# Chosen prototype weights turned by a DMA together with the weighed products, the search for the two nearest prototypes placed elsewhere, and the distances' roots by logarithm

## The chip, the cores and the metric

The kernel runs on one core of one Trainium2 chip. The metric is the device time of one execution in microseconds, from the median of several runs. The engines are TensorE (PE, matmuls; PEld its weight loads), VectorE (DVE), ScalarE (ACT), GpSimd (POOL) and SyncE (SP, which here issues most DMAs). Each runs its own instructions in order and waits on semaphores for the others.

## The reference, cut to what matters

Two layers, each a cross attention and a feed-forward part, on `x` of 64 x 256 tokens of 256 values:

```
x = x + tanh(g_xattn[0]) * L0_xattn(layernorm(x), ctx, ctx)
x = x + tanh(g_ffn[0])   * L0_ffn(layernorm(x))             # mixture of experts
x = x + tanh(g_xattn[1]) * L1_xattn(layernorm(x), ctx, ctx) # 16 heads of 64, 77 keys
x = x + tanh(g_ffn[1])   * L1_ffn(layernorm(x))
```

The change is in the last line. For each token `xf` and the 32 prototypes:

```
d2 = x2 + p2[None, :] - 2.0 * (xf @ prototypes.T)
dists = sqrt(maximum(d2, 0))
w = softmax(-dists / t); topw, topi = top_k(w, 2); topw = topw / sum(topw)
for tslot in range(2):                       # the two nearest prototypes
    h = einsum('nri,ni->nr', B[idx], xf)     # rank 16
    y = einsum('nor,nr->no', A[idx], h) + bias[idx]
    out = out + topw[:, tslot] * y
```

Of the softmax only the two nearest count, so the kernel needs their distances' gap alone.

## The kernel before

The second layer is `attention_ffn_phase`. It works on 64 batches of two tiles of 128 tokens (`TPB` is 2; h = 0 is the even tile of a batch and h = 1 the odd one). Its bodies are written out for the first and the last batches, and in a loop of 16 batches between them. A tile passes through a pipeline of eight steps; in the body of tile t each engine works at several tiles in a fixed order, which is the order written in `body` of each engine (lines 1207, 1338, 1458, 1607). Between the engines stand semaphores; `need(engine, semaphore, value)` is a wait.

For tile t the attention's scores are made. For tile t-1 they are made to exponentials (ScalarE) and half sums (GpSimd `softmax_sums`, L1143). For t-2 follow the inverse sums (VectorE, L1534) and the normalising (GpSimd, L1153). For t-3 TensorE turns the probabilities in three groups (L1442), ScalarE writes their high half (L1243) and VectorE their low half (`split_lo`, L1527), and attention adds the products with the values (L1454). For t-4 the second layer norm is made (ScalarE), split in two half-precision parts, the low one by GpSimd (`normed_low`, L1170), and turned by a DMA (L1089). For t-5 TensorE multiplies it with all 32 x 16 columns of `B` and with the prototypes (`low`, two banks); ScalarE copies the products, VectorE makes the distances' variable part (`dots`). Then, still in that body and as its last work but one, VectorE searches the two nearest of t-5 (`nearest_two`, `nearest_index`, L1569 to L1579).

For t-6 ScalarE makes the two squared distances (`square_gaps`, L1293); GpSimd adds a tiny number, takes the root as a power of 0.5, subtracts, and takes a power for the weights' ratio (`top_weights`, L1180). VectorE makes the two weights, compares a row of indices with each index found (`pick`, twice, L1658), and adds the two picks to `wsel`: three copies of the 32 weights side by side (L1665). For t-7 GpSimd multiplies `low` with the weights (`weigh`, L1194), ScalarE and GpSimd split the product in two halves (`hw_parts`, L1330 and L1175), and SyncE turns them by one DMA transpose of 8 blocks of 128 x 128 (L1095). `wsel` is turned on its own: TensorE transposes it into a bank (L1502), ScalarE copies 96 rows as half precision (L1384), and VectorE makes of the third copy the remainder (L1638): `wselT`. For t-8 TensorE multiplies `hwT` with `A` (12 matmuls) and `wselT` with the biases (L1486), and VectorE adds the result to the rows (L1627).

Five banks of the matrix engine's output memory go round among these uses (`Ring`, L84; `uses`, L981). Before TensorE fills a bank it waits for whoever read that bank's last use (`freed`, L998). The second half of `low` in an even tile takes the bank of the first group of the turned probabilities of the same tile. The second query block of an even tile takes the bank of the first half of `low`.

Once in a batch GpSimd also makes the low half of the normalised rows of the batch ahead (`rows_low`, L1165), at the start of an even tile.

The functions that the change touches:

Of the kernel before, what the change touches and what calls it, by code (L numbers as in the profile page):

```python
# [15 lines left out]
P = 128  # L16
# [67 lines left out]
class Ring:  # L84
# [3 lines left out]
    def __init__(self, uses, banks, first, last, steady):  # L88
        self.banks, self.steady = banks, steady
        self.flat, self.at_use = [], {}  # L90
        for i in range(first, last):
            for name in uses(i):
                self.at_use[i, name] = len(self.flat)
                self.flat.append((i, name))
        self.per = len(uses(steady))
        assert self.per % banks == 0
        tails = [uses(i)[-banks:] for i in (steady - 1, steady)]
        assert tails[0] == tails[1]

    def fill(self, i, name):  # L100

        n = self.at_use[i if isinstance(i, int) else self.steady, name]
        k = n // self.banks + 1
        return n % self.banks, k if isinstance(i, int) else (i - self.steady) * (self.per // self.banks) + k

    def before(self, i, name):

        n = self.at_use[i if isinstance(i, int) else self.steady, name] - self.banks
# [600 lines left out]
def attention_ffn_phase(nc, ctx, psum, const, src, src_rows, dst, keys, values, wq, score_scale, ffn, experts):  # L709
# [39 lines left out]
    SUM_STEPS, TOP_STEPS = 2, 4  # L749
# [28 lines left out]
    wsel_zero, euler_set, decay_ready = sem("wsel_zero"), sem("euler_set"), sem("decay_ready")  # L778
# [15 lines left out]
    gap_ready, ln_log, ln_root, more_ready, first_weight = sem("gap_ready"), sem("ln_log"), sem("ln_root"), sem("more_ready"), sem("first_weight")  # L794
# [5 lines left out]
    low_ready, hw_ready, hw_hi, hw_lo, wselT_hi, wselT_ready, out_ready = (  # L800
        sem("low_ready"), sem("hw_ready"), sem("hw_hi"), sem("hw_lo"), sem("wselT_hi"), sem("wselT_ready"),
        sem("out_ready"))
# [159 lines left out]
    wsel = sb("wsel", [P, P])  # L962
    wselT = sb("wselT", [BIAS_ROWS, P], F16)
    low = [sb(f"low{p}", [P, LOW]) for p in range(2)]
    hw = sb("hw", [P, LOW])
    hw_parts = sb("hw_parts", [P, 2, LOW], F16)
    hwT = [sb(f"hwT{p}", [P, 2 * LC, P], F16) for p in range(2)]
# [9 lines left out]
    def uses(i):  # L977

        names = []
        for h in range(TPB):  # L980
# [8 lines left out]
            names += of(7, [("wselT", h)])  # L989
# [6 lines left out]
    ring = Ring(uses, WORK, 0, END, BODIES)  # L996

    def freed(i, use):  # L998
# [11 lines left out]
        return (wselT_ready, t - 6) if what == "wselT" else (out_ready, t - 7)  # L1010
# [34 lines left out]
    def _(sp):  # L1045
# [45 lines left out]
        def turn_weighed(t, p):  # L1091
# [3 lines left out]
            sp.dma_start_transpose(hwT[p][:, :, :], flat(hw_parts[:, :, :])).then_inc(hwT_in[p], 16)  # L1095
# [30 lines left out]

        load_x(2, 2, 0)
# [9 lines left out]
    def _(pool):  # L1137
        pool.memset(wsel[:, :], 0.0).then_inc(wsel_zero, 1)
# [55 lines left out]
        def weigh(t, h):  # L1194
# [6 lines left out]
                               wsel[:, 0:NPROTO].unsqueeze(2).broadcast_to([P, NPROTO, RANK]), ALU.mult)\  # L1201
                .then_inc(hw_ready, 1)

        def body(i, u, j):
            for h in range(TPB):
# [23 lines left out]
    def _(act):  # L1229
# [63 lines left out]
        def square_gaps(t, h, u):  # L1293
# [3 lines left out]
            need(act, ysq_done, t + 1)  # L1297
            need(act, more_ready, t)
            act.activation(square[:, :], top[:, 0:2], ACT.Relu, bias=ysq[:, n:n + 1], scale=-1.0).then_inc(gap_ready, 1)
# [30 lines left out]
        def weighed_high(t, u, h, j):  # L1330

            need(act, hw_ready, t + 1)
            if live(t - 1, NT):
                earlier, times = turned_place(8, u, h, j)
                need(act, hwT_in[earlier], (times + 1) * 16)
            act.activation(hw_parts[:, 0, :], hw[:, :], ACT.Copy).then_inc(hw_hi, 1)

        def body(i, u, j):
            for h in range(TPB):
# [14 lines left out]
                if live(t - 6, NT):  # L1354
                    square_gaps(t - 6, h, u)
# [10 lines left out]
                if live(t - 4, NT):  # L1366
# [31 lines left out]
    def _(pe):  # L1398
# [67 lines left out]
        def body(i, u, j):  # L1466
            for h in range(TPB):
# [9 lines left out]
                if live(t - 8, NT):  # L1477
# [3 lines left out]
                    need(pe, wselT_ready, t - 7)  # L1481
# [4 lines left out]
                    filled(nc.tensor.matmul(bank[:, 0:D], wselT[:, :], ffn["bias"][:, :], start=False, stop=True),  # L1486
# [22 lines left out]
        pe.wait_ge(wsel_zero, 1)  # L1509
# [1519 lines left out]
```

## Time and profile before

| | us |
|---|---|
| median of 3 runs | 3023.89 |
| lowest and highest | 3023.6, 3030.8 |
| the profiled execution | 3015.37 |
| its span, first to last instruction | 3013.7 |
| TensorE busy | 2738.8 (91%) |
| VectorE busy | 2461.3 (82%) |
| ScalarE busy | 2199.1 (73%) |
| GpSimd busy | 2084.7 (69%) |

The second layer begins at about 1460 us and goes to the end. All times in the timelines are microseconds from the span's start. A line of a timeline is one or several like instructions: start, duration, engine and line, what is written and read, how many (x), and in brackets how long the engine had been idle before and who ended that. A merged line's duration runs to the end of its last instruction. Instructions of an engine overlap a little: the next often starts before the last one's recorded end. For a small instruction the distance between two starts is what it costs its queue. Names carry a prefix (`a_`), and buffer numbers are left out: some of TensorE's rows name a weight that shares its place.

### The profile page before, as it was taken

To read this page: it belongs to the slowest core of one execution; us is meant where nothing else is said; L and a number is where in the kernel's file an instruction comes from. 1 tells how busy PE (TensorE), PEld (TensorE's weight loads), DVE (VectorE), ACT (ScalarE), POOL (GpSimd) and SP (SyncE) were. 2 spreads that over 40 slices of the span, in tenths; PEclk is the share of its full clock that TensorE was granted. 3 is DMA by queue.
4 is the path that set the end of the run, shared out by engine and by line. 5 is a ranking of instruction groups with operands and counts; after the bars stand their busy time and mean duration, and the time that the engine had idled before them with its cause. 6 is when DMAs were issued, how large, how long until landed. Compare 5 with 4: busy or idle time off the path is not lost.

```text
span 3013.7 us, 96194 instructions
## 1 busy us (share of the span) xinstructions
PE 2738.8 (91%) x31534; PEld 2164.9 (72%) x31534; DVE 2461.3 (82%) x5870; ACT 2199.1 (73%) x5452; POOL 2084.7 (69%) x2777
## 2 busy tenths in 40 slices
PE   3889897899999999789799999999999999999996
PEld 2444444687778777657588888888888888888884
DVE  6787786688888888675589989888888888989884
ACT  2666666677777777575577777788877788778873
POOL 3893000576667666644378888888888888888886
PEclk7999999899999999999899999999999999999998
DMA  5997666223223223632467777677776777767763
GB/s 153 354 352 293 242 256 255 78 78 92 84 80 89 83 81 94 221 101 59 103 144 162 151 152 149 145 152 149 149 142 147 150 151 146 149 149 153 148 132 79
DMA packets 568793, 455.47 MB, mean 151 GB/s; under 512 B 383616, under 2 KB 527600, under 8 KB 555312
## 3 DMA queue, kind: packets, MB, share of 16 engines
q1 hardware_dynamic: 548144, 402.29, 53.2%
q0 software_dynamic: 7328, 23.40, 2.5%
q10 hardware_dynamic: 12960, 25.23, 2.3%
q8 instruction: 195, 3.19, 0.5%
q14 instruction: 166, 1.36, 0.2%
HBM read 235.08 MB, written 148.83 MB: 127 GB/s over the span
## 4 chain that ended last, share of the span: by engine, by line
PE 33%; DVE 10%; issue 4%; POOL 2%; DMA 1%; ACT 1%; SPq 0%; DVEq 0%; POOLq 0%; ACTq 0%
PE banks L150 10%; PE banks L152 9%; PE banks L151 9%; DVE a_pick L1658 2%; PE banks L1450 2%; DVE a_probT_lo L1527 2%; PE banks L1436 2%; DVE a_y L1604 1%; DVE a_rsum L1539 1%; DVE a_stats L1645 1%; DVE a_wtop L1597 1%; PE banks L1502 0%; DVE a_qT_lo L1525 0%; DVE a_smax L1546 0%; POOL a_pn L1160 0%
## 5 line engine op out<-in xcount | busy, mean ns | idle before, releaser
L383 POOL TENSOR_TENSOR a_probT_lo<-a_expT,a_probT_hi 128x512 f16<-128x512 f32 x256 | 291.5, 1160 | 218.4 <-ACT a_probT_hi L466 218.4
L459 ACT ACTIVATE a_expT<-banks,a_top,w_score_scale 128x512 f32<-128x512 f32 (+1 forms) x384 | 272.3, 709 | 152.4 <-PE banks L550 146.0
L1160 POOL TENSOR_TENSOR a_pn<-a_prob,a_rsum 128x1024 f32<-128x1024 f32 (+1 forms) x256 | 310.3, 1233 | 53.3 <-DVE a_rsum L1541 53.2
L1243 ACT ACTIVATE a_qT_hi<-banks 128x512 f16<-128x512 f32 x252 | 149.8, 595 | 210.1 <-PE banks L152 210.1
L150 PE MATMUL banks<-a_xnT,w_q_hi 128*128 128x256 f16 x1024 | 281.9, 275 | 15.8 <-DMA a_xnT<-a_xn_parts 13.9
L150 PE MATMUL banks<-a_vo_front,a_probT_hi 128*128 128x256 f16 x1024 | 279.5, 273 | 9.6 <-DVE a_probT_lo L1527 3.6
L151 PE MATMUL banks<-a_xnT,w_q_hi 128*128 128x256 f16 x1024 | 281.7, 275 | 0.0
L152 PE MATMUL banks<-a_xnT,w_q_lo 128*128 128x256 f16 x1024 | 281.5, 275 | 0.0
L152 PE MATMUL banks<-a_vo_front,a_probT_lo 128*128 128x256 f16 x1024 | 279.3, 273 | 0.0
L151 PE MATMUL banks<-a_vo_front,a_probT_hi 128*128 128x256 f16 x1024 | 279.3, 273 | 0.0
L1243 ACT ACTIVATE a_probT_hi<-banks 128x512 f16<-128x512 f32 (+1 forms) x384 | 193.8, 517 | 42.2 <-PE banks L1450 41.3
L1525 DVE TENSOR_TENSOR a_qT_lo<-banks,a_qT_hi 128x512 f16<-128x512 f32 x252 | 172.3, 684 | 45.5 <-ACT a_qT_hi L1243 40.7
L550 PE MATMUL banks<-ident,a_shifted 128*128 128x128 f32 (+1 forms) x1280 | 204.4, 284 | 5.3
L1527 DVE SCALAR_TENSOR_TENSOR a_probT_lo<-banks,a_probT_hi 128x512 f16<-128x512 f32 (+1 forms) x384 | 206.9, 581 | 0.3 <-ACT a_probT_hi L1243 0.3
L2397 DVE SCALAR_TENSOR_TENSOR kv_vo_out<-banks,kv_vo_out 128x512 f16<-128x512 f32 (+1 forms) x312 | 191.6, 679 | 16.5 <-ACT kv_vo_out L2295 16.5
L1450 PE MATMUL banks<-ident,a_pn 128*128 128x128 f32 (+1 forms) x1280 | 197.6, 278 | 2.0 <-issue 2.0
L659 DVE TENSOR_TENSOR a_shifted<-banks,a_smax 128x1024 f32<-128x1024 f32 (+1 forms) x256 | 192.2, 793 | 3.8
L2295 ACT ACTIVATE kv_vo_out<-banks 128x512 f16<-128x512 f32 (+1 forms) x312 | 172.4, 603 | 29.4 <-DMA vo<-kv_vo_out 22.1
L150 PE MATMUL banks<-w_downT_hi,a_ynT 128*128 128x288 f16 (+1 forms) x512 | 145.0, 283 | 47.5 <-DVE a_probT_lo L1527 45.1
L1199 POOL TENSOR_TENSOR a_hw<-a_low,a_wsel 128x512 f32<-128x512 f32 x128 | 135.4, 1058 | 72.7 <-DVE a_wsel L1665 72.7
L649 DVE TENSOR_REDUCE a_smax<-banks 128x16 f32<-128x1232 f32 x128 | 183.6, 1435 | 2.2 <-PE banks L536 1.9
L1278 ACT ACTIVATE a_prob<-banks,a_third_shift,w_score_scale 128x77 f32<-128x77 f32 x512 | 170.7, 414 | 12.0 <-ACT a_third_shift L1273 0.4
(383 smaller groups left out, 10315.9 us busy)
## 6 DMA issues: line engine op xcount, KB each, us to landing
vo<-kv_vo_out SPq DMA_DIRECT2D x38, 2048.0 KB, 7.8
a_vo_front<-vo SPq DMA_DIRECT2D x128, 512.0 KB
kt<-kv_k_out ACTq DMA_DIRECT2D x9, 2560.0 KB, 15.0
a_k<-kt SPq DMA_DIRECT2D x64, 308.0 KB, 3.4
kv_raw_e<-in_L_ffn_w POOLq DMA_DIRECT2D x16, 1024.0 KB, 8.8
a_x<-in_x SPq DMA_DIRECT2D x64, 256.0 KB, 2.9
a_y<-in_x SPq DMA_DIRECT2D x64, 256.0 KB, 2.7
x<-a_y SPq DMA_DIRECT2D x64, 256.0 KB, 2.8
```

The source lines that it names most:

```text
L150: nc.tensor.matmul(out, lhs[0], rhs[0], start=start, stop=False)
L151: nc.tensor.matmul(out, lhs[0], rhs[1], start=False, stop=False)
L152: return nc.tensor.matmul(out, lhs[1], rhs[0], start=False, stop=stop)
L383: pool.tensor_tensor(probT[b][1][:, first:end, :], expT[b][:, first:end, :], probT[b][0][:, first:end, :], ALU.subtract).then_inc(prob_rea ...
L459: act.activation(expT[1 - h][0:rows, first:end, :], bank, ACT.Exp, bias=top[0:rows, 0:1], scale=weights["score_scale"][0:rows, 0:1]).then_ ...
L550: last = nc.tensor.transpose(bank[0:rows, c * P:(c + 1) * P], shifted[1 - h][:, place:place + rows], ident[:, :])
L659: last = nc.vector.tensor_tensor(shifted[h][:, cols].rearrange("p (r h k) -> p r h k", r=TILES, k=end - first), held_scores[:, :, :, first ...
L1160: last = pool.tensor_tensor(keys_of(pn[h]), e[:, :, first:end].rearrange("p (a c) k -> p a c k", a=outer), rsum[h][:, :].rearrange("p (a c ...
L1243: act.activation(out, bank[:, 0:cols].rearrange("p (c s) -> p c s", c=out.shape[1]), ACT.Copy, scale=scale)\
L1450: last = nc.tensor.transpose(bank[0:rows, c * P:(c + 1) * P], turned, ident[:, :])
L1527: nc.vector.scalar_tensor_tensor(out=lo, in0=bank, scalar=scale, in1=hi, op0=ALU.mult, op1=ALU.subtract)\
L2397: nc.vector.scalar_tensor_tensor(out=vo_out[q][0:m, placed(b), 1, :], in0=product_banks(g, c, b, m), scalar=1.0 / OUT_TOP, in1=vo_out[q][0 ...
```

## The change

1. `wsel` becomes [128, 32], one copy of the weights. ScalarE writes two half-precision copies of it (`wsel_parts[:, 0:2]`) and GpSimd the remainder (`wsel_parts[:, 2]`), right behind the split products in one row `hw_all` of 9 x 128 columns; 32 columns at its end are zeroed once, and SyncE waits for that at its start. The DMA transpose turns 9 blocks in place of 8, and the bias matmul takes its weights from the ninth. TensorE's transpose of `wsel`, ScalarE's copy of it and VectorE's remainder leave. VectorE's `wsel` waits for the last tile's split (`hw_lo`) in place of `wselT_ready` and `hw_ready`.
2. The bank of that transpose stays in the ring as a spare that nobody fills: the next use of the bank waits for the use before the spare.
3. VectorE's search of a tile moves from the end of one body to the next body, behind the three low halves of the probabilities and ahead of the scores' maximum.
4. ScalarE's `square_gaps` moves behind the length of the normed rows (`length2`) and ahead of their high half. Behind that half comes the logarithm of the squares (`log_gaps`), with the tiny number as its bias, and behind the copies of `low` the exponential of half of it (`root_gaps`).
5. GpSimd's `top_weights` loses the addition and the power; it waits for `dist_ready`. It now stands behind `normed_low`.

The core of the diff (the parts of `Ring`, of the semaphores' names and of the tiles' sizes are left out):

```diff
@@ SyncE
-            sp.dma_start_transpose(hwT[p][:, :, :], flat(hw_parts[:, :, :])).then_inc(hwT_in[p], 16)
+            sp.dma_start_transpose(hwT[p][:, :, :], hw_all[:, :]).then_inc(hwT_in[p], 16)
...
+        sp.wait_ge(pad_zero, 1)
@@ GpSimd
-        pool.memset(wsel[:, :], 0.0).then_inc(wsel_zero, 1)
+        pool.memset(hw_all[:, 2 * LOW + BIAS_ROWS:], 0.0).then_inc(pad_zero, 1)
...
             need(pool, hw_hi, t + 1)
+            pool.tensor_tensor(wsel_parts[:, 2, :], wsel[:, :], wsel_parts[:, 0, :], ALU.subtract)
             pool.tensor_tensor(hw_parts[:, 1, :], hw[:, :], hw_parts[:, 0, :], ALU.subtract).then_inc(hw_lo, 1)
...
-            need(pool, gap_ready, t + 1)
-            kept = pool.tensor_tensor(dist[:, :], square[:, :], numbers[:, 2:3].broadcast_to([P, 2]), ALU.add)
+            need(pool, dist_ready, t + 1)
+            gap = pool.tensor_tensor(dgap[:, :], dist[:, 1:2], dist[:, 0:1], ALU.subtract)
             pool.tensor_copy(topf[:, :], topi[:, 0:2]).then_inc(top_ready, 1)
-            step(kept)
-            step(pool.tensor_tensor(dist[:, :], dist[:, :], numbers[:, 1:2].broadcast_to([P, 2]), ALU.pow))
-            step(pool.tensor_tensor(dgap[:, :], dist[:, 1:2], dist[:, 0:1], ALU.subtract))
+            step(gap)
             step(pool.tensor_tensor(late[:, :], decay[:, :], dgap[:, :], ALU.pow))
...
+                if live(t - 4, NT):
+                    normed_low(t - 4)
                 if live(t - 6, NT):
                     top_weights(t - 6)
-                if live(t - 4, NT):
-                    normed_low(t - 4)
@@ ScalarE
+        def log_gaps(t):
+            need(act, gap_squared, t + 1)
+            act.activation(square[:, :], square[:, :], ACT.Ln, bias=numbers[:, 2:3]).then_inc(gap_log, 1)
+        def root_gaps(t):
+            need(act, gap_log, t + 1)
+            need(act, more_ready, t)
+            act.activation(dist[:, :], square[:, :], ACT.Exp, scale=0.5).then_inc(dist_ready, 1)
...
+            act.activation(wsel_parts[:, 0:2, :], wsel[:, :].unsqueeze(1).broadcast_to([P, 2, NPROTO]), ACT.Copy)
             act.activation(hw_parts[:, 0, :], hw[:, :], ACT.Copy).then_inc(hw_hi, 1)
...
-                if live(t - 6, NT):
-                    square_gaps(t - 6, h, u)
                 if live(t - 4, NT):
                     norm2_root(t - 4)
...
                     length2(t - 4, h, u)
+                if live(t - 6, NT):
+                    square_gaps(t - 6, h, u)
+                if live(t - 4, NT):
                     normed_high(t - 4, u, h, j)
+                if live(t - 6, NT):
+                    log_gaps(t - 6)
...
-                if live(t - 7, NT):
-                    bank = full(i, ("wselT", h))
-                    act.activation(wselT[:, :], bank[0:BIAS_ROWS, 0:P], ACT.Copy).then_inc(wselT_hi, 1)
+                if live(t - 6, NT):
+                    root_gaps(t - 6)
@@ TensorE
-                    need(pe, wselT_ready, t - 7)
...
-                    filled(nc.tensor.matmul(bank[:, 0:D], wselT[:, :], ffn["bias"][:, :], start=False, stop=True),
+                    filled(nc.tensor.matmul(bank[:, 0:D], hwT[turned][0:BIAS_ROWS, 2 * LC, :], ffn["bias"][:, :], start=False, stop=True),
                            i, ("ffn", h))
...
-                if live(t - 7, NT):
-                    need(pe, wsel_ready, t - 6)
-                    bank = bank_for(i, ("wselT", h))
-                    filled(nc.tensor.transpose(bank[:, 0:P], wsel[:, :], ident[:, :]), i, ("wselT", h))
@@ VectorE
+                if live(t - 6, NT):
+                    nearest_two(t - 6)
+                    nearest_index(t - 6)
                 if live(t, NT):
                     maximum(t)
...
-                if live(t - 7, NT):
-                    bank, rows = full(i, ("wselT", h)), slice(2 * NPROTO, BIAS_ROWS)
-                    need(dve, wselT_hi, t - 6)
-                    nc.vector.tensor_tensor(wselT[rows, :], bank[rows, 0:P], wselT[rows, :], ALU.subtract)\
-                        .then_inc(wselT_ready, 1)
...
-                    need(dve, wselT_ready, t - 6)
-                    need(dve, hw_ready, t - 6)
-                    nc.vector.tensor_tensor(wsel[:, 0:BIAS_ROWS].rearrange("p (r n) -> p r n", r=3),
-                                            pick[:, 0, :].unsqueeze(1).broadcast_to([P, 3, NPROTO]),
-                                            pick[:, 1, :].unsqueeze(1).broadcast_to([P, 3, NPROTO]), ALU.add)\
-                        .then_inc(wsel_ready, 1)
-                if live(t - 5, NT):
-                    nearest_two(t - 5)
-                    nearest_index(t - 5)
+                    need(dve, hw_lo, t - 6)
+                    nc.vector.tensor_tensor(wsel[:, :], pick[:, 0, :], pick[:, 1, :], ALU.add).then_inc(wsel_ready, 1)
```

## Rows read from the trace of the kernel before

**Rows 1.** The page's first line.

```profile
span 3013.7 us, 96194 instructions
```

**Rows 2.** Busy time by engine in a stretch: length, PE, PEld, DVE, ACT, POOL, clock, DMA.

```profile
1600.00:2900.00 1300.00, 1250.08 (x15296) 1082.09 (x15294) 1155.26 (x3284) 1033.98 (x3096) 1136.15 (x1604) 1.00 0.72 149
```

**Rows 3.** Waits of TensorE from 1600 to 2900 us: total, times, longest.

```profile
PE banks L150 <- DVE a_probT_lo L1527: 41.4, 55, 1.6
```

**Rows 4.** Timeline of TensorE: start, duration, line, output<-input, count, [idle before <-releaser].

```profile
2104.96 0.27 PE L1502 MATMUL banks<-ident,a_wsel 128*128 128x128 f32 x1
...
2111.89 0.27 PE L150 MATMUL banks<-w_upT_hi,a_hwT 128*128 128x256 f16 x1
...
2114.98 0.28 PE L150 MATMUL banks<-w_downT_hi,a_ynT 128*128 128x256 f16 x1 [0.77 <-DVE a_probT_lo L1527]
...
2115.64 0.27 PE L1502 MATMUL banks<-ident,a_wsel 128*128 128x128 f32 x1
2115.99 0.28 PE L150 MATMUL banks<-a_vo_front,a_probT_hi 128*128 128x256 f16 x1
```

**Rows 5.** Timeline of VectorE in the same batch.

```profile
2109.86 0.48 DVE L1604 SCALAR_TENSOR_TENSOR a_y<-banks,out_scale,a_y 128x256 f32<-128x256 f32 x1 [1.43 <-PE banks L152]
...
2111.20 1.71 DVE L1658 TENSOR_SCALAR a_pick<-iota,a_topf,a_wtop 128x32 f32<-128x32 f32 x2
2112.95 0.26 DVE L1665 TENSOR_TENSOR a_wsel<-a_pick 128x96 f32<-128x96 f32 x1
2113.13 0.19 DVE L1574 MAX8 a_top<-a_dots 128x8 f32<-128x32 f32 x1
...
2113.55 0.42 DVE L1539 TENSOR_REDUCE a_rsum<-a_quarter 128x16 f32<-128x256 f32 x1
...
2114.23 1.62 DVE L1527 SCALAR_TENSOR_TENSOR a_probT_lo<-banks,a_probT_hi 128x512 f16<-128x512 f32 x3
```

**Rows 6.** Timeline of GpSimd in the same batch.

```profile
2105.11 1.16 POOL L1178 TENSOR_TENSOR a_hw_parts<-a_hw,a_hw_parts 128x512 f16<-128x512 f32 x1 [0.48 <-ACT a_hw_parts L1336]
...
2107.28 0.19 POOL L1190 TENSOR_TENSOR a_dgap<-a_dist 128x1 f32<-128x1 f32 x1
...
2108.34 0.67 POOL L1173 TENSOR_TENSOR a_yn_parts<-a_yn,a_yn_parts 128x256 f16<-128x256 f32 x1
2108.97 1.30 POOL L1148 TENSOR_TENSOR a_half<-a_prob 128x512 f32<-128x512 f32 x1
...
2111.72 1.15 POOL L1168 TENSOR_TENSOR a_xn_parts<-a_xn,a_xn_parts 128x512 f16<-128x512 f32 x1
```

**Rows 7.** Timeline of ScalarE in the same batch.

```profile
2103.77 0.19 ACT L1291 ACTIVATE a_rstd<-a_vare 128x1 f32<-128x1 f32 x1
2103.86 0.19 ACT L1255 ACTIVATE a_minus_mean<-a_mv 128x2 f32<-128x2 f32 x1
2103.95 0.28 ACT L1256 ACTIVATE a_vare<-a_mv,eps 128x2 f32<-128x2 f32 x1
2104.14 0.28 ACT L1304 ACTIVATE a_shift<-a_minus_mean,a_rstd 128x1 f32<-128x1 f32 x1
...
2106.95 0.26 ACT L1384 ACTIVATE a_wselT<-banks 96x128 f16<-96x128 f32 x1
2107.11 0.59 ACT L1243 ACTIVATE a_qT_hi<-banks 128x512 f16<-128x512 f32 x1
...
2110.32 0.63 ACT L1320 ACTIVATE a_xn_parts<-a_xn 128x512 f16<-128x512 f32 x1
```

**Rows 8.** Timeline of SyncE's queue: transposes of the weighed products, mid-loop and at the end.

```profile
2106.44 1.27 SPq L1095 DMA_TRANSPOSE a_hwT<-a_hw_parts  x1
...
2983.52 1.23 SPq L1095 DMA_TRANSPOSE a_hwT<-a_hw_parts  x1
...
3003.45 1.23 SPq L1095 DMA_TRANSPOSE a_hwT<-a_hw_parts  x1
```

**Rows 9.** Tile hwT, its transposes' time to landing, all 128.

```profile
DMA to landing us min/median/max: 3.0/3.1/6.3
```

More of the change, by code:

```diff
@@ L84, with __init__ @@
 class Ring:
-    def __init__(self, uses, banks, first, last, steady):
-        self.banks, self.steady = banks, steady
+    def __init__(self, uses, banks, first, last, steady, spare=None):
+        self.banks, self.steady, self.spare = banks, steady, spare
         self.flat, self.at_use = [], {}
+        filled = [0] * banks
         for i in range(first, last):
             for name in uses(i):
-                self.at_use[i, name] = len(self.flat)
+                filled[len(self.flat) % banks] += name[0] != spare
+                self.at_use[i, name] = len(self.flat), filled[len(self.flat) % banks]
                 self.flat.append((i, name))
-        self.per = len(uses(steady))
-        assert self.per % banks == 0
+        kept = uses(steady)
+        assert len(kept) % banks == 0
+        start = self.at_use[steady, kept[0]][0]
+        self.per = [sum(name[0] != spare for name in kept[(s - start) % banks::banks]) for s in range(banks)]
         tails = [uses(i)[-banks:] for i in (steady - 1, steady)]
@@ L100, in fill @@
     def fill(self, i, name):
-        n = self.at_use[i if isinstance(i, int) else self.steady, name]
-        k = n // self.banks + 1
-        return n % self.banks, k if isinstance(i, int) else (i - self.steady) * (self.per // self.banks) + k
+        n, k = self.at_use[i if isinstance(i, int) else self.steady, name]
+        s = n % self.banks
+        return s, k if isinstance(i, int) else (i - self.steady) * self.per[s] + k
     def before(self, i, name):
-        n = self.at_use[i if isinstance(i, int) else self.steady, name] - self.banks
+        n = self.at_use[i if isinstance(i, int) else self.steady, name][0] - self.banks
+        while n >= 0 and self.flat[n][1][0] == self.spare:
+            n -= self.banks
         if n < 0:
@@ L961, in attention_ffn_phase @@
     pick = sb("pick", [P, 2, NPROTO])
-    wsel = sb("wsel", [P, P])
-    wselT = sb("wselT", [BIAS_ROWS, P], F16)
+    wsel = sb("wsel", [P, NPROTO])
     low = [sb(f"low{p}", [P, LOW]) for p in range(2)]
     hw = sb("hw", [P, LOW])
-    hw_parts = sb("hw_parts", [P, 2, LOW], F16)
-    hwT = [sb(f"hwT{p}", [P, 2 * LC, P], F16) for p in range(2)]
+    TURNED = 2 * LC + 1
+    hw_all = sb("hw_all", [P, TURNED * P], F16)
+    hw_parts = hw_all[:, 0:2 * LOW].rearrange("p (s n) -> p s n", s=2)
+    wsel_parts = hw_all[:, 2 * LOW:2 * LOW + BIAS_ROWS].rearrange("p (r n) -> p r n", r=3)
+    hwT = [sb(f"hwT{p}", [P, TURNED, P], F16) for p in range(2)]
     first_x = [sb(f"first_x{n}", [P, D]) for n in range(FIRST_X)]
@@ L988, in uses @@
             names += of(5, [("low", h, n) for n in range(LU)])
-            names += of(7, [("wselT", h)])
+            names += of(7, [("spare", h)])
             names += prep(4)
@@ L994, in uses @@
         return names
-    ring = Ring(uses, WORK, 0, END, BODIES)
+    ring = Ring(uses, WORK, 0, END, BODIES, "spare")
     def freed(i, use):
@@ L1009, in freed @@
             return y_ready, t - 2
-        return (wselT_ready, t - 6) if what == "wselT" else (out_ready, t - 7)
+        return out_ready, t - 7
     def bodies(eng, body):
@@ L1200, in weigh @@
                                low[h][:, :].rearrange("p (n r) -> p n r", n=NPROTO),
-                               wsel[:, 0:NPROTO].unsqueeze(2).broadcast_to([P, NPROTO, RANK]), ALU.mult)\
+                               wsel[:, :].unsqueeze(2).broadcast_to([P, NPROTO, RANK]), ALU.mult)\
                 .then_inc(hw_ready, 1)
@@ L1297, in square_gaps @@
             need(act, ysq_done, t + 1)
+            act.activation(square[:, :], top[:, 0:2], ACT.Relu, bias=ysq[:, n:n + 1], scale=-1.0).then_inc(gap_squared, 1)
+        def log_gaps(t):
[3 more added lines that the diff above has]
+            need(act, gap_log, t + 1)
             need(act, more_ready, t)
-            act.activation(square[:, :], top[:, 0:2], ACT.Relu, bias=ysq[:, n:n + 1], scale=-1.0).then_inc(gap_ready, 1)
+            act.activation(dist[:, :], square[:, :], ACT.Exp, scale=0.5).then_inc(dist_ready, 1)
         def norm2_shift(t):
```

15 lines of the change are left out of this document (6 added, 9 removed).

## The prediction

> **What bounds the kernel now.** The profiled execution took 3015.4 us, its span is 3013.7 [rows 1]; the median of the runs shown is 3023.9, 8.5 above it. The sums below are made in the profiled execution, and the 8.5 is added at the end. The change lies in the second layer's loop, 64 batches of two tiles. I read the busy times of a stretch in the middle of that loop first: of 1300 us TensorE is busy 1250, at a granted clock of 1.00 (its 2.4 GHz level), all others less [rows 2]. So TensorE sets the pace except where it waits. The waits come next: one large group, 41.4 us in 55 waits, so one in each batch of 1300 / 55 = 23.6 us, released by the VectorE line that writes the probabilities' low halves [rows 3].
>
> The timeline of one batch shows where. I call the tile whose `low` products come at 2104 the odd tile (h = 1), the next one the even tile (h = 0). In the even tile the second half of `low` starts after 0.77 us of idleness. The turn of `wsel` follows at 2115.64 and attention at 2115.99, 0.35 later; attention needs the last low half, which ends at 2114.23 + 1.62 = 2115.85. In the pipeline a matmul or a turn takes 0.11 us (six from 2114.98 to 2115.64; a row's 0.27 is the latency), so 0.24 of the 0.35 is waiting. Together TensorE loses 0.77 + 0.24 = 1.01 us a batch to VectorE [rows 4].
>
> Then backwards along VectorE [rows 5]. It idles 1.43 us before the residual at 2109.86, so its lateness begins after that. The two picks begin at 2111.20 and end only at 2112.91. On GpSimd the low half of the next batch's rows runs 2111.72 to 2112.87 [rows 6]: the second pick ends 0.04 after it. So the loop that sets the end of a batch is: GpSimd's `top_weights`, `normed_low`, `softmax_sums`, `rows_low`; then pick, `wsel`, search, inverse sums, low halves on VectorE; then attention on TensorE. GpSimd in turn was released by ScalarE at 2105.11, after an idle 0.48, and ScalarE by TensorE's third turn of probabilities.
>
> **The change, part by part.**
>
> *Search moved behind the low halves.* From its first instruction, 2113.13, to the inverse sums, 2113.55, it holds VectorE 0.42 us, in the loop. It now runs after the low halves, on no one's path to attention: 0.42 gained. In its new place it stands in front of the maximum and of the reading of the prototype products. Both follow the same chain, so what is gained ahead of the low halves covers it: they come 0.86 earlier by the sum below and 0.42 later by the search. If that cover is gone, TensorE's second query block, which takes the bank of these products, waits.
>
> *`wsel` from 96 to 32 columns.* 0.26 us now; the inverse sums' 256 columns take 0.42 [rows 5], which makes 1.0 ns a column and 0.06 for 64. Bounds 0 and 0.13 (half); I take 0.06.
>
> *GpSimd.* The addition and the power leave; in the loop they take 2106.22 to 2107.28, from the end of `weighed_low` at 2105.11 + 1.11 to the subtraction [rows 6]. The low half of `wsel`, 32 columns, comes in front of `weighed_low`: between nothing and the 0.19 of the subtraction; I take 0.15. `normed_low` moves ahead of `top_weights`, which changes no sum but starts its transpose 2 us earlier. Without a wait, `softmax_sums` would start 1.06 - 0.15 = 0.9 earlier. But `top_weights` now waits for ScalarE's root.
>
> *ScalarE.* Between the third high half and the root: the square leaves its old place and returns before the low products' copies, no change. Added are the copy of `wsel` to two halves, 64 columns, and the logarithm. A logarithm of two columns takes 0.19 in the queue (2103.95 to 2104.14), an exponential 0.09 (2103.77 to 2103.86) though it lasts 0.19; the copy I put at 0.15, by the copy of `wselT`, 0.16 in the queue (2106.95 to 2107.11) for 128 columns; it could be 0.09 to 0.30 [rows 7]. The root takes the place of that copy: it starts at 2106.95 + 0.15 + 0.19 = 2107.29 and ends at 2107.48. GpSimd's subtraction then starts at 2107.53, with 0.05 for the release; from there to the end of the group is 2108.34 - 2107.28 = 1.06, so `softmax_sums` starts at 2108.59 in place of 2108.97: 0.38 gained, and most of the 0.9 is lost in the wait. Queued behind the waiting subtraction are only `top_weights` and `softmax_sums`. If the copy and the logarithm cost their full durations (0.26, 0.28) the gain falls to 0.18; if the release is late too, to nothing or a loss of 0.1. The other end is the 0.9 of a root that is there in time. ScalarE as a whole gets 0.15 + 0.19 + 0.09 - 0.16 = 0.27 later, so the high half that `rows_low` needs ends at 2110.95 + 0.27 = 2111.22; GpSimd reaches `rows_low` at 2111.72 - 0.38 = 2111.34. It just does not wait.
>
> *TensorE.* Two turns of `wsel` leave, 0.22 a batch. The even tile's lies before the attention, which waits for VectorE anyway; the odd tile's lies outside the loop above (it leaves TensorE at the third turn of probabilities and comes back at the even tile's attention). So while the stall stays they are worth nothing. They raise the most that can be had: 1.01 + 0.22 = 1.23 a batch. The bias matmul and the banks' order stay; the spare bank frees nothing that was waited for.
>
> *VectorE's low half of `wselT`* leaves too. It lies outside the loop, since VectorE catches up anyway in its 1.43 of idleness: nothing.
>
> *The transpose of nine blocks in place of eight.* It is issued at 2106.44, lands 3.1 later, 2109.5, and TensorE uses it at 2111.89 [rows 4, 8, 9]: 2.3 us of slack. One block more makes at most 3.1 x 9/8 = 3.5, and 0.15 later for GpSimd's addition. Nothing; without cover it would be 1 us for each us.
>
> *Start and end.* The wait of SyncE for the memset at the start replaces others, under 1 us either way. At the end the last tiles run one after another, 6.6 us each (four issues from 2983.52 to 3003.45 [rows 8]). There each tile gets longer by the copy 0.15, GpSimd's subtraction 0.15 and the ninth block 0.2: 0.5, five times, 2.5 us. Bounds 0 and 6.
>
> **Sum.** 0.42 + 0.06 + 0.38 = 0.86 us a batch. It counts in some 61 batches of 64, without those in which the pipeline fills and drains: 52.5 us. Less 2.5: 50 faster. 3015.4 - 50 = 2965.4, and with the 8.5 between profile and median, 2974.
>
> **The rivals.**
>
> *A pick gets ahead of `rows_low`.* GpSimd starts `rows_low` by my numbers 0.12 after its input is there. If ScalarE's additions are a little dearer, or GpSimd a little faster, there is a gap between its two instructions in which the second pick runs first. Then VectorE gains nearly the whole of `rows_low`'s 1.15 on top, the stall is gone, and TensorE's 1.23 is the gain: 61 x 1.23 - 2.5 = 72.5, 2951. For it speaks how narrow the 0.12 is; against it that `softmax_sums`, which holds the first pick back in the same way, would have to end before the input of `rows_low` is there.
> The Trainium skill (SBUF — State Buffer, "Who interferes with whom") says that such a VectorE instruction and a GpSimd one exclude each other and whoever issues first holds the pair for its whole length. By that rule, and the trace agrees with the 0.04 above, the order of the two decides and not their lengths.
>
> *The gain on GpSimd does not come.* The chain search, square, logarithm, root, subtraction, power crosses three engines inside one tile. If the root comes 0.4 later than I have it, only 0.48 a batch is left: 61 x 0.48 - 2.5 = 27, 2997. For it speaks that I know ScalarE's additions only from neighbours.
>
> *Slower: the ninth block.* An odd number of blocks might not go at the price of the others. The place is the odd tile's transpose, used by the even tile's `ffn`. From there to attention TensorE needs 2115.64 - 2111.89 - 0.77 = 2.98. Attention is later than now only if the landing takes more than 2115.99 - 2.98 - 2106.59 = 6.4 us. The longest landing so far is 6.3 [rows 9]; with 9/8 of that, 7.1 each time, it is 0.7 a batch slower, 61 x 0.7 + 2.5 = 45, 3069. Against it: the median landing is 3.1 and the lowest 3.0, so hardly anything moves it now.
>
> *The relief is filled by other waits* (the query bank, a bank freed by `ffn`'s addition): within 0.3%, 3024.
>
> **How the numbers follow.** Forecast 0.46, own range 2962 to 2986 (the copy and the logarithm at their two ends). Pick ahead 0.28; no gain on GpSimd 0.16; filled by other waits 0.05; slower 0.05. 0.3% is 9 us, about what a measurement of this kernel can tell from no change. The first three are faster by more: 0.90; the same 0.05; slower 0.05. The range takes in the first three with their bounds: 2945 is 64 x 1.23 = 79 with no loss at the end; 3004 is 61 x 0.38 - 2.5 = 20.5, where GpSimd's part turns to a loss of 0.1. So 2945 to 3005.
>
> **What would show it.** In the profile after: TensorE's wait for the low halves smaller than 41.4 (by my sum 1.23 - 0.86 = 0.37 a batch are left, ahead of attention rather than in `low`); a batch 0.86 us shorter; the search between low halves and maximum; `softmax_sums` starting 1.1 after the root ends; the second pick still ending with `rows_low`. It is wrong if a batch gets more than 1.1 shorter (the pick was ahead), if GpSimd starts `softmax_sums` no earlier after the third high half than now, or if TensorE shows waits for the transposed weights.

## The result, and the profile after

| | before, us | after, us |
|---|---|---|
| median | 3023.95 | 2976.54 |
| lowest and highest | 3023.6, 3030.8 | 2971.54, 2977.84 |
| the profiled execution | 3015.37 | 2975.93 |
| its span | 3013.7 | 2973.9 |

The ratio is 0.9839, with a 95% interval of 0.9825 to 0.9853. The kernel became 1.6% faster. The forecast was 2974, with a range of 2945 to 3005. The medians differ by 47.4 us and the two profiled executions by 39.4. The same kernel on another chip gave 0.9851 (0.9834 to 0.9869).

The first line of the page, and TensorE's wait for the low halves from 1600 to 2860 us (total, times, longest), to be set beside [rows 1, 3]:

```profile
span 2973.9 us, 95792 instructions
```

```profile
PE banks L156 <- DVE a_probT_lo L1541: 25.4, 103, 0.5
```

The wait fell from 41.4 to 25.4 us, and it is now met about twice in a batch. TensorE's timeline shows both places, the second half of `low` and attention. The first row is the third turn of probabilities in the odd tile, where ScalarE and GpSimd start from:

```profile
2086.26 0.43 PE L1470 MATMUL banks<-ident,a_pn 128*104 128x128 f32 x2
...
2098.20 0.29 PE L158 MATMUL banks<-w_downT_hi,a_ynT 128*128 128x288 f16 x1
2098.88 0.28 PE L156 MATMUL banks<-w_downT_hi,a_ynT 128*128 128x256 f16 x1 [0.39 <-DVE a_probT_lo L1541]
...
2099.43 0.27 PE L158 MATMUL banks<-w_downT_hi,a_ynT 128*128 128x256 f16 x1
2099.88 0.28 PE L156 MATMUL banks<-a_vo_front,a_probT_hi 128*128 128x256 f16 x1 [0.18 <-DVE a_probT_lo L1541]
```

In `low` 0.39 us of idleness are left of the 0.77 [rows 4]. From the last matmul of `low` to attention it is 0.45, so 0.34 of waiting beside the 0.11 that a matmul takes, where it was 0.24. Together that is 0.73 a batch, from 1.01.

The idle times 0.77 and 0.39 begin only at the recorded end of the matmul ahead, so its latency hides a part of the waiting. That matmul in the kernel before:

```profile
2113.93 0.29 PE L152 MATMUL banks<-w_downT_hi,a_ynT 128*128 128x288 f16 x1
```

From start to start it is 2114.98 - 2113.93 = 1.05 before and 2098.88 - 2098.20 = 0.68 now, of which such a matmul takes 0.12 in the pipeline. So TensorE loses 0.93 there before and 0.56 now, and with attention 1.17 a batch before and 0.90 now. The difference hardly changes, but the prediction's 1.01, and with it the most that can be had, was 0.16 too small.

VectorE in the same batch, from the residual to the search in its new place:

```profile
2094.13 0.48 DVE L1618 SCALAR_TENSOR_TENSOR a_y<-banks,out_scale,a_y 128x256 f32<-128x256 f32 x1 [1.10 <-PE banks L158]
...
2095.31 0.57 DVE L1611 TENSOR_TENSOR a_wtop<-a_late,a_wtop 128x1 f32<-128x1 f32 x1
2095.91 1.31 DVE L1670 TENSOR_SCALAR a_pick<-iota,a_topf,a_wtop 128x32 f32<-128x32 f32 x2
2097.25 0.19 DVE L1676 TENSOR_TENSOR a_wsel<-a_pick 128x32 f32<-128x32 f32 x1
2097.45 0.42 DVE L1553 TENSOR_REDUCE a_rsum<-a_quarter 128x16 f32<-128x256 f32 x1
...
2098.13 1.62 DVE L1541 SCALAR_TENSOR_TENSOR a_probT_lo<-banks,a_probT_hi 128x512 f16<-128x512 f32 x3
2099.67 0.19 DVE L1588 MAX8 a_top<-a_dots 128x8 f32<-128x32 f32 x1
```

Against [rows 5]: from the end of the picks to the inverse sums it took 2113.55 - 2112.91 = 0.64 and now takes 2097.45 - 2097.22 = 0.23. The line of the farther weight lasts 0.57. In the kernel before it lasted 0.12:

```profile
2111.04 0.12 DVE L1597 TENSOR_TENSOR a_wtop<-a_late,a_wtop 128x1 f32<-128x1 f32 x1
```

GpSimd in the same batch: `normed_low`, the subtraction, the first half sum, the last one, `rows_low`:

```profile
2090.77 0.67 POOL L1181 TENSOR_TENSOR a_yn_parts<-a_yn,a_yn_parts 128x256 f16<-128x256 f32 x1
2091.99 0.19 POOL L1195 TENSOR_TENSOR a_dgap<-a_dist 128x1 f32<-128x1 f32 x1 [0.55 <-ACT a_dist L1316]
...
2093.05 1.30 POOL L1156 TENSOR_TENSOR a_half<-a_prob 128x512 f32<-128x512 f32 x1
...
2095.25 0.62 POOL L1159 TENSOR_TENSOR a_quarter<-a_quarter,a_prob 128x208 f32<-128x208 f32 x1
2095.82 1.15 POOL L1176 TENSOR_TENSOR a_xn_parts<-a_xn,a_xn_parts 128x512 f16<-128x512 f32 x1
```

The farther weight ends when the last half sum has ended (2095.87), the first pick can start only at 2095.91, and `rows_low` has begun at 2095.82. So both picks now stand behind it. They end 0.25 after it; before, only the second stood there and ended 0.04 after it [rows 5, 6].

ScalarE: the copy of `wsel`, the weighed products, the logarithm and its neighbour, the root and its neighbour:

```profile
2088.61 0.24 ACT L1353 ACTIVATE a_hw_all<-a_wsel 128x64 f16<-128x64 f32 x1
2088.76 0.61 ACT L1354 ACTIVATE a_hw_all<-a_hw 128x512 f16<-128x512 f32 x1
...
2090.54 0.28 ACT L1310 ACTIVATE a_square<-a_square,a_numbers 128x2 f32<-128x2 f32 x1
2090.73 0.47 ACT L1274 ACTIVATE a_shift<-a_minus_mean,a_rstd 128x1 f32<-128x1 f32 x2
...
2091.63 0.19 ACT L1316 ACTIVATE a_dist<-a_square 128x2 f32<-128x2 f32 x1
2091.72 0.58 ACT L1250 ACTIVATE a_qT_hi<-banks 128x512 f16<-128x512 f32 x1
```

The copy costs its queue 0.15, the logarithm 0.19, the root 0.09.

The time a batch takes in us, from one odd tile's residual to the next (starts in VectorE's timeline; the residuals in the timelines above are those of even tiles, with the same period in mid-loop), by stretch, and the kernels of the experiments beside it. Batch 1 is the first with a residual in both tiles; during the first 13 VectorE also adds the first layer's expert outputs.

| kernel | start of batch 1 | 1-13 | 14-28 | 29 | 30-43 | 44-59 | 60-63 | rest |
|---|---|---|---|---|---|---|---|---|
| before | 1508.3 | 23.71 | 23.35 | 23.31 | 23.63 | 23.18 | 21.56 | 35.5 |
| after | 1513.6 | 22.58 | 22.83 | 22.80 | 22.99 | 22.62 | 20.45 | 35.8 |
| after, other chip | 1511.2 | 22.58 | 22.83 | 22.80 | 23.00 | 22.62 | 20.55 | 35.7 |
| search back | 1512.9 | 23.27 | 23.18 | 23.16 | 23.47 | 23.02 | 20.56 | 35.7 |
| power back | 1509.9 | 23.16 | 23.10 | 23.07 | 23.29 | 22.88 | 21.12 | 36.6 |
| turns kept | 1510.6 | 22.59 | 22.84 | 22.82 | 23.33 | 22.64 | 20.33 | 35.8 |
| rows later | 1511.7 | 22.41 | 22.52 | 23.19 | 22.84 | 22.35 | 20.18 | 37.2 |
| rows behind picks | 1503.9 | 22.48 | 22.12 | 22.00 | 22.41 | 21.93 | 20.13 | 35.8 |
| turn alone | 1508.8 | 23.47 | 23.45 | 23.41 | 23.71 | 23.28 | 21.26 | 36.6 |
| twelve blocks | 1512.7 | 22.60 | 22.83 | 22.82 | 23.00 | 22.63 | 20.46 | 37.6 |
| rows behind, turns kept | 1514.5 | 22.60 | 22.23 | 22.11 | 22.72 | 22.15 | 20.54 | 35.8 |
| before, rows behind picks | 1509.9 | 23.14 | 22.53 | 22.39 | 22.78 | 22.74 | 21.50 | 34.4 |

From the first column on, the span fell by 45 us: 14.7 in batches 1 to 13, 8.4 in 14 to 29, 17.9 in 30 to 59, 4.4 in the last four, and 0.4 back at the end. Ahead of that column nothing was changed, and yet it differs by up to 11 us among these profiles. So spans are compared less surely than batches.

In batch 30 the loop turns back. It took 27.35 us before and 25.18 after. Busy times around it (length, PE, PEld, DVE, ACT, POOL, granted clock, DMA) of the kernel before, of the changed one, and of the experiment with the turns kept, where this batch took 29.33:

```profile
2190.00:2218.00 28.00, 25.42 (x279) 21.49 (x278) 20.48 (x61) 18.86 (x56) 22.68 (x33) 0.88 0.65 133
```

```profile
2172.00:2198.00 26.00, 23.01 (x283) 19.98 (x282) 19.98 (x60) 18.96 (x60) 20.18 (x30) 1.00 0.76 146
```

```profile
2169.00:2200.00 31.00, 26.90 (x292) 22.53 (x291) 20.97 (x62) 19.48 (x62) 22.72 (x34) 0.89 0.77 136
```

The granted clock stayed at 1.00 there (the 2.4 GHz level) in three of the twelve profiles, the two of the changed kernel and that with twelve blocks, and the batch took 25.2 to 25.3 us. In the other nine it fell for a part of the batch, which took 25.8 to 29.3. So the 2.2 us of this batch can't be put down to the loop of the theory alone. Why the clock fell in some kernels and not in others is not shown.

### The profile page after: what moved, and what is told of

The parts are those of the page before. It is cut to its first block and busy times, and to the rows that moved or that the text cites. A ratio compares the mean times of both kernels' runs of the same rounds, so it can differ in the third digit from the quotient of the medians.

```text
span 2973.9 us, 95792 instructions
## 1 busy us (share of the span) xinstructions
PE 2718.9 (91%) x31406; PEld 2150.3 (72%) x31406; DVE 2397.3 (81%) x5742; ACT 2224.4 (75%) x5708; POOL 1998.5 (67%) x2649
## 5 line engine op out<-in xcount | busy, mean ns | idle before, releaser
L1156 POOL TENSOR_TENSOR a_half<-a_prob 128x512 f32<-128x512 f32 x128 | 166.0, 1297 | 15.5 <-ACT a_prob L1371 15.3
```

## The experiments

All are told against the changed kernel; their ratios are to the kernel before, on their own chip, where it took 3015 to 3017 us. The theory is the loop of the prediction: GpSimd's `rows_low` holds the picks, VectorE is late for the low halves, TensorE waits for them.

**The search back at the end of the body.**

```diff
-                if live(t - 6, NT):          # ahead of maximum(t)
-                    nearest_two(t - 6)
-                    nearest_index(t - 6)
...
+                if live(t - 5, NT):          # behind wsel
+                    nearest_two(t - 5)
+                    nearest_index(t - 5)
```

> The changed kernel with the search for the nearest two back at the end of the body, behind wsel, everything else as changed. Theory (the batch's end is set by a loop over GpSimd's rows_low, the picks, VectorE's work up to the low halves, and attention): the search's 0.42 us stand in the loop again, a batch becomes 0.42 longer, 61 x 0.42 = 26 us, so about 3002 against the changed kernel's 2976, ratio to the kernel before 0.993. Rival (what the change gave came from TensorE's 0.22 and from the work that leaves, the place of the search is indifferent): 2976 to 2980, ratio 0.984 to 0.986.

Measured: 3001.03 us, ratio 0.9937 (0.992 to 0.9955). The wait for the low halves (from 1600 to 2860 us, as in the next three experiments):

```profile
PE banks L156 <- DVE a_probT_lo L1541: 50.5, 106, 1.6
```

A batch is 0.35 longer in batches 14 to 29 and 0.69 in the first 13: 24.5 us in all where 26 were expected, and the rival is out.

**The roots on GpSimd again.**

```diff
-            need(pool, dist_ready, t + 1)
+            need(pool, gap_squared, t + 1)
+            kept = pool.tensor_tensor(dist[:, :], square[:, :], numbers[:, 2:3].broadcast_to([P, 2]), ALU.add)
...
+            step(kept)
+            step(pool.tensor_tensor(dist[:, :], dist[:, :], numbers[:, 1:2].broadcast_to([P, 2]), ALU.pow))
...
-                    log_gaps(t - 6)
-                    root_gaps(t - 6)
```

> The changed kernel with the distances' roots on GpSimd again, by addition and power, and no logarithm and exponential on ScalarE; the order of GpSimd's work stays as changed. Theory (the same loop): GpSimd no longer waits for ScalarE's root (0.55 us in each odd tile of the changed kernel) but takes 1.06 for the two instructions, so softmax_sums starts 0.46 to 0.5 later, and the second pick with it: 61 x 0.48 = 29 us, about 3005, ratio 0.994. Rival (GpSimd's start is no part of what sets the batch): not slower than 2979, or faster, since ScalarE is relieved of 0.28 a tile: ratio 0.983 to 0.985.

Measured: 2995.87 us, ratio 0.9924 (0.9911 to 0.9938).

```profile
PE banks L156 <- DVE a_probT_lo L1540: 33.3, 101, 0.7
```

VectorE's picks, then GpSimd's `softmax_sums`, last half sum and `rows_low`, in the batch whose residual starts at 2101.32:

```profile
2102.88 1.78 DVE L1669 TENSOR_SCALAR a_pick<-iota,a_topf,a_wtop 128x32 f32<-128x32 f32 x2
```

```profile
2100.71 1.30 POOL L1156 TENSOR_TENSOR a_half<-a_prob 128x512 f32<-128x512 f32 x1
...
2102.91 0.61 POOL L1159 TENSOR_TENSOR a_quarter<-a_quarter,a_prob 128x208 f32<-128x208 f32 x1
2103.47 1.16 POOL L1176 TENSOR_TENSOR a_xn_parts<-a_xn,a_xn_parts 128x512 f16<-128x512 f32 x1
```

Slower, as the theory has it, but a batch in the middle is 0.27 longer and not 0.48. `softmax_sums` does start 0.47 later against the residual (0.61 ahead of it instead of 1.08). But with GpSimd later, the first pick gets ahead of `rows_low` again, so the second ends at 3.34 after the residual instead of 3.09.

**One more turn a tile on TensorE.** It turns the unit matrix and nobody reads it.

```diff
+                if live(t - 7, NT):
+                    bank = bank_for(i, ("spare", h))
+                    nc.tensor.transpose(bank[:, 0:P], ident[:, :], ident[:, :])
                 prep(4)
```

> The changed kernel with one more 128 x 128 turn (of the unit matrix, into the spare bank, read by nobody) on TensorE in each tile, at the place where the turn of wsel was. Theory: while TensorE waits 0.7 us a batch for the low halves, its own 0.22 are worth nothing: within 3 us of the changed kernel, ratio 0.983 to 0.985. Rival (TensorE is 96% busy and sets the pace): 61 x 0.22 = 13 us slower, 2990, ratio 0.988.

Measured: 2977.34 us, ratio 0.9863 (0.9845 to 0.9881), the changed kernel 0.9839 (0.9825 to 0.9853) and on another chip 0.9851. Its median is 0.8 us above that of the changed kernel, where the rival had 13.

```profile
PE banks L156 <- DVE a_probT_lo L1544: 9.8, 35, 0.4
```

The batches take what they take without the turns (22.84 against 22.83), and the wait gets shorter as it is filled. Batches 30 to 43 differ (23.33): 4.7 us in all, 4.1 of it in batch 30, where the granted clock fell in this run and not in the changed kernel's. The 0.22 us are worth nothing while the wait is there.

**`rows_low` behind `weigh`.**

```diff
-                if h == 0 and live(i + 1, NB):
-                    rows_low(i + 1)
                 if live(t - 7, NT):
                     weigh(t - 7, 1 - h)
+                if h == 0 and live(i + 1, NB):
+                    rows_low(i + 1)
```

> The changed kernel with GpSimd's rows_low (the low half of the next batch's rows) behind weigh in place of ahead of it. weigh waits for wsel and so for the picks; then rows_low can't hold the picks back any more. Theory: the picks end 1.0 us earlier against the residual, VectorE reaches the low halves 0.9 earlier, and TensorE's 0.73 of waiting in each batch goes: 61 x 0.7 = 43 us faster than the changed kernel, 2934, ratio 0.970. Rivals: weigh, the normalising and the transpose of the rows come later (1.15 us at most), and that shows as TensorE waits for the turned rows or for the probabilities, with most of the gain lost: 2960 to 2976; or the picks were never held by rows_low but by VectorE's own chain: 2976.

Measured: 2961.27 us, ratio 0.9816 (0.9799 to 0.9832). The wait for the low halves is no longer in the list; a new one leads it:

```profile
PE banks L156 <- DMA a_xnT<-a_xn_parts: 13.7, 16, 1.5
```

Most batches take 22.2 us and about one in four takes 23.1. The picks were held by `rows_low`, but of the 43 us that the theory had, only 15 came (2961 against 2934 forecast): a part of the gain went into the wait for the turned rows, which the expectation had as a rival.

**`rows_low` ahead of `weigh`, but behind both picks.**

```diff
                 if h == 0 and live(i + 1, NB):
+                    if live(t - 7, NT):
+                        need(pool, picked, t - 6)
                     rows_low(i + 1)
```

> The changed kernel with GpSimd's rows_low still ahead of weigh, but waiting for both picks. In the run with rows_low behind weigh the good batches took 22.2 us (changed kernel: 22.8) and one in three or four took 23.1, with TensorE waiting for the turned rows. Theory: the picks are free as there, and the rows' low half ends 1.1 us earlier than there, so the waits for the turned rows go and all batches take 22.2: 61 x 0.6 = 37 us faster than the changed kernel, about 2938, ratio 0.972. Rival 1: weigh is now 1.1 later, the high half of the weighed products and all that ScalarE does behind it come later too, and that costs TensorE something: 2945 to 2960. Rival 2: the long batches had another cause than the turned rows: as rows_low behind weigh, ratio 0.981.

Measured: 2940.37 us, ratio 0.9755 (0.9737 to 0.9773). TensorE's wait for the low halves (here and in the two lists below from 1600 to 2820 us), then VectorE and GpSimd in one batch:

```profile
PE banks L156 <- DVE a_probT_lo L1543: 2.1, 10, 0.2
```

```profile
2096.83 0.48 DVE L1620 SCALAR_TENSOR_TENSOR a_y<-banks,out_scale,a_y 128x256 f32<-128x256 f32 x1 [1.10 <-PE banks L158]
...
2098.01 0.57 DVE L1613 TENSOR_TENSOR a_wtop<-a_late,a_wtop 128x1 f32<-128x1 f32 x1
2098.62 0.50 DVE L1672 TENSOR_SCALAR a_pick<-iota,a_topf,a_wtop 128x32 f32<-128x32 f32 x2
2099.16 0.19 DVE L1678 TENSOR_TENSOR a_wsel<-a_pick 128x32 f32<-128x32 f32 x1
```

```profile
2097.95 0.62 POOL L1159 TENSOR_TENSOR a_quarter<-a_quarter,a_prob 128x208 f32<-128x208 f32 x1
2099.28 1.16 POOL L1176 TENSOR_TENSOR a_xn_parts<-a_xn,a_xn_parts 128x512 f16<-128x512 f32 x1 [0.71 <-DVE a_pick L1672]
2100.40 1.06 POOL L1206 TENSOR_TENSOR a_hw<-a_low,a_wsel 128x512 f32<-128x512 f32 x1
```

The farther weight is still held by the last half sum, but both picks then take 0.50 together, and `rows_low` starts behind them. They end 2099.12 - 2096.83 = 2.29 after the residual, 0.8 earlier than in the changed kernel. The wait for the turned rows, 13.7 us in the experiment before, is no longer in the list. A batch takes 22.00. What is left of TensorE's waiting stands ahead of attention:

```profile
2101.57 0.27 PE L158 MATMUL banks<-w_downT_hi,a_ynT 128*128 128x256 f16 x1
2101.78 0.28 PE L156 MATMUL banks<-a_vo_front,a_probT_hi 128*128 128x256 f16 x1
```

That is 0.21 - 0.11 = 0.10. The account closes from start to start: 1.17 of waits and 0.22 of turns less these 0.10 are 1.29, and 23.29 - 1.29 = 22.00. The prediction's 1.23 would end at 22.06 with no wait left, so it was too small. This version beats both kernels.

**The turn by DMA alone**, with search and roots as before (the first two edits above together, on the changed kernel; `normed_low` stays ahead of `top_weights`).

> The kernel before with the turn of the chosen weights by the DMA alone (and normed_low ahead of top_weights): the search at the end of the body, the roots on GpSimd by addition and power, as before. Theory (loop over GpSimd and VectorE, TensorE waits 1.0 us in it): VectorE's narrower wsel gives 0.06 a batch, GpSimd's low half of wsel costs 0.15 to 0.2, TensorE's 0.22 are worth nothing: 0 to 9 us slower than the kernel before, ratio 1.000 to 1.003. Rival (TensorE sets the pace): 61 x 0.22 = 13 us faster, ratio 0.9955.

Measured: 3018.79 us, ratio 1.0009 (0.9999 to 1.002).

```profile
PE banks L156 <- DVE a_probT_lo L1540: 59.6, 102, 1.6
```

No gain: a batch in the middle is 0.10 longer than before. TensorE has 0.22 less to do and waits longer instead.

**Twelve blocks in the transpose.**

```diff
-    TURNED = 2 * LC + 1
+    TURNED = 2 * LC + 4
```

> The changed kernel with 12 blocks of 128 x 128 in the transpose in place of 9 (three more of zeros, used by nobody). From 8 to 9 blocks the median landing went from 3.1 to 3.4 us. Theory: 0.3 a block, so the landing is about 4.3, and the 2.3 us of slack hide it: same as the changed kernel within 3 us, ratio 0.984, and 3 us more at the end where tiles run one after another. Rival (more transpose traffic delays the other DMAs, or blocks are dearer beyond some number): TensorE waits for hwT, 2985 and more.

Measured: 2975.2 us, ratio 0.9862 (0.9844 to 0.9881). The transposes' landing, first of the changed kernel (9 blocks), then of this one (12):

```profile
DMA to landing us min/median/max: 3.2/3.4/5.4
```

```profile
DMA to landing us min/median/max: 3.7/3.9/5.6
```

The medians are 3.1 us for 8 blocks [rows 9], 3.4 for 9 and 3.9 for 12, where 4.3 was expected. The batches are unchanged to 0.02; the end, where tiles run one after another, is 1.9 longer, where 3 was expected.

**The changed kernel again.**

> The changed kernel itself, for a comparison on one chip with the others of this call: ratio to the kernel before 0.984 as measured, 2969 to 2977.

Measured: 2971.11 us, ratio 0.9851 (0.9834 to 0.9869), all batches to 59 equal to 0.01.

**`rows_low` behind the picks, and the additional turns.** The edits of both.

> The kernel with rows_low behind the picks (2940, ratio 0.9755, TensorE hardly waits) with the additional turn of the unit matrix in each tile, which cost the changed kernel nothing. Theory: what hid it there was TensorE's wait for the low halves; that is gone, so the two turns cost their 0.22 a batch: 22.22 in place of 22.00, 61 x 0.22 = 13 us, about 2953, ratio 0.980. Rival (a turn runs in a gap of its own in any case): as without, 0.9755.

Measured: 2952.58 us, ratio 0.978 (0.9767 to 0.9794). 12 us more than without the turns, on another chip (by the ratios 7.5, and the two intervals touch), and a batch in the middle 0.11 to 0.22 longer. The theory's direction, with half its size in the best stretch: the even tile's turn takes the place of the 0.10 that was left of the wait ahead of attention, and 0.22 - 0.10 = 0.12 is about the 0.11 measured.

**The kernel before, with `rows_low` behind the picks.** The same edit on the kernel before.

> The kernel before with nothing changed but rows_low waiting for both picks. Theory: in the odd tile the second pick ends at 2.25 after the residual in place of 3.05, 0.8 us earlier, and TensorE's 1.01 of waiting shrinks by as much: a batch takes 22.5 in place of 23.3, 61 x 0.8 = 49 us, ratio 0.984, the same gain as that of the whole change. Rival (rows_low holds the picks only because of what the change did, or the DVE search must leave first): ratio 0.995 to 1.000.

Measured: 2978.79 us, ratio 0.9872 (0.9857 to 0.9887).

```profile
PE banks L150 <- DMA a_hwT<-a_hw_parts: 4.9, 8, 1.2
PE banks L150 <- DVE a_probT_lo L1529: 2.7, 5, 0.7
```

A batch takes 22.39 in its best stretch, 0.9 less; in the first and the late batches it gains half of that, so the ratio stays behind the 0.984 expected. TensorE now waits for the turned products at times, but whether that is the other half is left open. The rival is out. One additional wait on GpSimd is worth most of what the whole change is.

## Why the prediction was right, point by point

*Where the time was.* Right. TensorE's wait for the low halves was the one that paid, though it was 1.17 us a batch and not 1.01. The runs show it from four sides: the search alone and the roots alone move the batch, a turn more on TensorE doesn't, and the turn less doesn't either.

*The search, 0.42, and `wsel`, 0.06.* Together 0.48 forecast, 0.64 - 0.23 = 0.41 measured behind the picks. `wsel` fell from 0.26 to 0.19. With the search back a batch is 0.35 longer.

*GpSimd, 0.38.* From the third turn of probabilities to `softmax_sums` it was 2108.97 - 2101.88 = 7.09 ([rows 6] and the row below) and is 2093.05 - 2086.26 = 6.79: 0.30 gained. TensorE's third turn in the kernel before:

```profile
2101.88 0.43 PE L1450 MATMUL banks<-ident,a_pn 128*104 128x128 f32 x2
```

The pieces on ScalarE came as worked out (0.15, 0.19, 0.09); the subtraction started 0.08 later than I had it, and from there to `softmax_sums` it took 1.06, as forecast. The wait on the root ate the larger part of the 0.9, as said: and with the power back on GpSimd the whole gain from the roots is 0.27 a batch, since the picks then fall better between GpSimd's instructions.

*The picks.* This is the step that was mis-sized, by 0.21 of the 0.86: "the second pick ends 0.04 after it", carried over unchanged. With GpSimd earlier against VectorE, the farther weight, one column, met the last half sum and was held, 0.57 in place of 0.12. The first pick came too late to run between the two GpSimd instructions, and both ended behind `rows_low`, 0.25 after it. That is 0.21 lost. The sum in mid-loop is so 0.28 (`rows_low` ends 10.71 after the third turn, from 10.99) + 0.41 - 0.21 = 0.48, where 0.86 stood. Measured: 2116.94 - 2094.13 = 22.81, from 23.29: 0.48.

*Why the total is right all the same.* That is luck in part. The 46 batches from 14 to 59 gave 26.3 us, 2.2 of them in batch 30, where the clock fell before and not after; the other 45 gave 0.54 each. The first 13 gave 1.13 each. There VectorE adds the expert outputs, behind `wsel` and the search. Before, this came just after GpSimd had begun `weigh`, and was held (VectorE, then GpSimd, of the kernel before):

```profile
1617.33 1.08 DVE L1692 SCALAR_TENSOR_TENSOR a_first_x<-a_first_y,a_first_w,a_first_x 128x256 f32<-128x256 f32 x1
```

```profile
1617.08 1.06 POOL L1199 TENSOR_TENSOR a_hw<-a_low,a_wsel 128x512 f32<-128x512 f32 x1 [0.62 <-DVE a_wsel L1665]
```

After, with the search gone from between, it is issued ahead of `weigh` (VectorE, then GpSimd, of the changed kernel):

```profile
1617.82 0.48 DVE L1697 SCALAR_TENSOR_TENSOR a_first_x<-a_first_y,a_first_w,a_first_x 128x256 f32<-128x256 f32 x1
```

```profile
1617.98 1.23 POOL L1206 TENSOR_TENSOR a_hw<-a_low,a_wsel 128x512 f32<-128x512 f32 x1 [0.55 <-DVE a_wsel L1676]
```

1.08 became 0.48, and GpSimd's instruction 1.06 became 1.23. So much is seen in one of four tiles, 0.3 a batch; with the search back these batches lose 0.69 of their 1.13. Elsewhere the hold got dearer: the additions of the bias, eight of them in the other tile of a batch, took 0.50 in the middle before and 0.90 after. These batches got shorter all the same, so those additions seem to be outside the loop. The rest of what these 13 batches gained more than the others I have not taken apart. So errors went against each other: 50 us were forecast, 45 came in the traces from batch 1 on, by another division. The part ahead of batch 1, where nothing was changed, was 5.3 longer in this profile, so the profiled executions differ by only 39.4. The 8.5 us that I added for the distance of profile and median did not recur (2975.9 and 2976.5), and that too happened to close the gap.

*The rival with the pick ahead.* It didn't occur, but it named the right lever. Forced by a wait, it gives 22.00 a batch and 2940 us, against the 2951 forecast for it. Its 1.23 a batch was too small, since TensorE's waiting in `low` was counted from the end of a matmul and not from where the next could have started; 1.29 came and 0.10 was left.

*The turns, the ninth block, the end.* Nothing, nothing, and 0.4 us in place of 2.5. The slower case had a landing of 7.1 us; it is 3.4, and 5.4 at most.

## What to carry to other kernels

When two engines exclude each other, look at the order in which their instructions are issued, not at their lengths: a short instruction on the path that ends the batch must not be issued behind a long one whose result is needed much later, and one wait on the right semaphore can put it in front. Work that is removed counts only on the loop that binds; follow that loop back through all engines before pricing an edit. A right total doesn't confirm the terms: compare the loop's period stretch by stretch, and look at the granted clock of a stretch before its time is put down to the change. What a wait costs a pipelined engine is read from start to start, not from the idle time that a row shows.

## What the runs showed of the hardware

A VectorE addition or product with two inputs in the core's memory is held by a running GpSimd instruction even with one column: 0.57 us against 0.12, and 1.08 against 0.48 with 256 columns. The Trainium skill (SBUF — State Buffer, "Who interferes with whom") says that an instruction with two such inputs contends with a GpSimd one that reads there, and that the one issued first holds the pair. The traces agree for VectorE. For GpSimd they agree in direction: its `weigh` took 1.23 in place of 1.06 where VectorE was first, 0.17 more, though the two rows overlap by 0.32 (1617.98 to 1618.30).

The picks, with one such input of 32 columns, were held as well: the two took 1.31 us together beside `rows_low`, and 0.50 where GpSimd was made to wait.

Two GpSimd instructions that follow each other leave room for one VectorE instruction that is already waiting, and for none that comes 0.09 us after the second has started (both seen with the picks and `rows_low`). A DMA transpose gets dearer by little: 0.3 us more to landing for the ninth block, 0.17 for each of three more.
